# Five subtractions of the first layer's end by way of ScalarE and GpSimd, and one normalisation on VectorE

## The reference

```python
x = x + tanh(g_xattn[0]) * attention0(layernorm(x), ctx, ctx, pos, mask)   # 32 heads in 8 groups, rotary positions
x = x + tanh(g_ffn[0])   * experts0(layernorm(x))                          # 16 experts, the best 2 of each token
x = x + tanh(g_xattn[1]) * attention1(layernorm(x), ctx, mask)             # RMS-normed queries and keys
x = x + tanh(g_ffn[1])   * lora_experts1(layernorm(x))                     # 4 experts of rank 16, the best 2
# attention: q = x @ Wq; k = ctx @ Wk; v = ctx @ Wv
#            scores = q k^T / sqrt(128), masked; probs = softmax(scores); out = (probs v) @ Wo
```

## Time and profile before

| | |
|---|---|
| median of 3 runs | 1198.05 us (1197.17 to 1198.39) |
| profiled execution, its own time | 1198.88 us |
| span of its records | 1196.8 us |
| TensorE busy | 1182.5 us, 99% of the span |
| VectorE busy | 825.7 us, 69% |
| GpSimd busy | 580.8 us, 49% |
| ScalarE busy | 423.9 us, 35% |
| subtractions into `o_lo` (L1431) | 128 of 682 ns mean, all on VectorE |

### The profile page before, as it was taken

The page is one execution under the profiler, slowest core; times in us unless marked ns, Lnnn a source line. Parts: engine busy times, 40 slices in busy tenths (PEclk is TensorE's granted clock), DMA queues, the critical chain, the costliest instruction groups (busy, mean ns, idle before and its releaser), DMA issues.

```text
span 1196.8 us, 16826 instructions
## 1 busy us (share of the span) xinstructions
PE 1182.5 (99%) x6178; PEld 944.8 (79%) x6178; DVE 825.7 (69%) x1454; ACT 423.9 (35%) x746; POOL 580.8 (49%) x396
## 2 busy tenths in 40 slices
PE   9999999999999999999999999999999999999998
PEld 7888888777778777777788888777777777777776
DVE  4656546888888888888973226766676767657795
ACT  5145152222213222222451115544443343544432
POOL 5522533766767576676463112336364554545500
PEclk9999999999999999999999999999999999999999
DMA  7844635712212221211211003112221221211101
GB/s 281 260 146 166 205 112 163 282 49 79 79 53 75 83 79 45 78 45 54 88 63 36 1 1 134 40 62 71 81 87 44 79 73 59 70 53 40 75 1 71
DMA packets 57314, 106.54 MB, mean 89 GB/s; under 512 B 3632, under 2 KB 36528, under 8 KB 51888
## 3 DMA queue, kind: packets, MB, share of 16 engines
q1 hardware_dynamic: 56736, 104.82, 25.4%
q0 software_dynamic: 384, 1.05, 0.2%
q10 hardware_dynamic: 144, 0.00, 0.0%
HBM read 78.59 MB, written 27.26 MB: 88 GB/s over the span
## 4 chain that ended last, share of the span: by engine, by line
PE 89%; DVE 7%; POOL 2%; issue 1%; ACT 1%; DVEq 0%; POOLq 0%; ACTq 0%
PE ps_q L225 13%; PE ps_b L225 13%; PE ps_b L227 13%; PE ps_b L226 13%; PE ps_q L226 12%; PE ps_q L227 12%; PE ps_s L938 4%; PE ps_b L965 4%; PE ps_q L925 1%; PE ps_s L273 1%; PE ps_q L2039 1%; PE ps_b L472 1%; DVE ln_buf L265 1%; PE ps_q L522 0%; PE ps_s L1733 0%
## 5 line engine op out<-in xcount | busy, mean ns | idle before, releaser
L225 PE MATMUL ps_q<-hT_hi,wq_hi 128*128 128x512 f32 x512 | 206.3, 403 | 0.0
L226 PE MATMUL ps_q<-hT_lo,wq_hi 128*128 128x512 f32 x512 | 199.8, 390 | 0.0
L227 PE MATMUL ps_q<-hT_hi,wq_lo 128*128 128x512 f32 x512 | 199.4, 389 | 0.0
L225 PE MATMUL ps_b<-wo_hi,o_hi 128*128 128x512 f32 x440 | 171.5, 390 | 0.7 <-POOL wo_lo L1256 0.7
L226 PE MATMUL ps_b<-wo_lo,o_hi 128*128 128x512 f32 x440 | 171.2, 389 | 0.0
L227 PE MATMUL ps_b<-wo_hi,o_lo 128*128 128x512 f32 x440 | 171.2, 389 | 0.0
L1431 DVE TENSOR_TENSOR o_lo<-ps_b,o_hi 128x512 fp32r<-128x512 f32 x128 | 82.0, 682 | 63.6 <-ACT o_hi L1141 62.3
L225 PEld LDWEIGHTS ps_q<-hT_hi,wq_hi 128*128 128x128 f32 x512 | 96.0, 188 | 33.2 <-issue 11.2
L1263 POOL TENSOR_TENSOR qT<-q_t 128x512 f32<-128x512 f32 x64 | 89.9, 1405 | 65.8 <-DVE q_t L1366 59.8
L1442 DVE SCALAR_TENSOR_TENSOR x_sb<-ps_b,gates,x_sb 128x512 f32<-128x512 f32 x117 | 83.8, 723 | 43.7 <-PE ps_b L227 43.3
L731 POOL TENSOR_TENSOR wq_lo<-wq_raw,wq_hi 128x512 fp32r<-128x512 f32 x64 | 90.3, 1415 | 47.8 <-ACT wq_hi L725 47.8
(11 more groups left out here) (272 smaller groups left out, 2471.5 us busy)
## 6 DMA issues: line engine op xcount, KB each, us to landing
wq_raw<-in_wq SPq DMA_DIRECT2D x16, 1024.0 KB, 4.8
wo_raw<-in_wo SPq DMA_DIRECT2D x16, 1024.0 KB, 4.8
kT<-kT_spill SPq DMA_DIRECT2D x32, 256.0 KB, 3.7
v_hi<-v_hi_spill SPq DMA_DIRECT2D x16, 512.0 KB, 3.7
v_lo<-v_lo_spill SPq DMA_DIRECT2D x16, 512.0 KB, 4.6
v_hi_spill<-vs_hi SPq DMA_DIRECT2D x12, 512.0 KB, 5.4
v_lo_spill<-vs_lo SPq DMA_DIRECT2D x12, 512.0 KB, 6.7
kw_raw<-in_wk SPq DMA_DIRECT2D x4, 1024.0 KB, 7.1
```

The costliest lines, as they stand in the source:

```text
L225: nc.tensor.matmul(dst, l_hi, r_hi, start=first, stop=False)
L226: nc.tensor.matmul(dst, l_hi, r_lo, start=False, stop=False)
L227: return nc.tensor.matmul(dst, l_lo, r_hi, start=False, stop=last)
```

## The change

It does three things, all in the first layer's end.

- Five low parts of value banks leave VectorE: 2 and 3 of unit 13, and 0, 2 and 3 of unit 14. For each, ScalarE copies the PSUM bank into a free slot of `wo_raw` (`out_copy`, signal `o_copied`), and GpSimd subtracts `o_hi` from that copy (`out_low` of `att_pool`, signal `o_back`). Low part 1 of unit 14 and all of unit 15 stay on VectorE.
- The normalisation of unit 14 (`att_normalise`) moves from GpSimd's stream to VectorE's, right behind the reciprocal.
- The waits follow: TensorE's `project_out` counts `o_back` where it counted `o_lo`, each copy waits until its slot is free, and ScalarE's first copy of the next stage's up weights waits for all five subtractions.

```diff
+        BY_POOL = 5
...
             def project_out(u, h, g, t):
                 if t % 2 == 0:
                     pe.wait_ge(*c("o_hi", 4 * u + t + 2))
-                    pe.wait_ge(*c("o_lo", 4 * u + t + 2))
+                    at_end = u - (2 * G - 3) if lay == 0 and isinstance(u, int) else -1
+                    if at_end < 0 or (at_end, t) == (0, 0):
+                        pe.wait_ge(*c("o_lo", 4 * u + t + 2))
+                    elif (at_end, t) == (1, 0):
+                        pe.wait_ge(*c("o_lo", 4 * u - 1))
+                        pe.wait_ge(c["o_back"], 3)
+                    elif at_end == 2:
+                        pe.wait_ge(*c("o_lo", 4 * u + t + 2 - BY_POOL))
+                    else:
+                        pe.wait_ge(c["o_back"], 2 if at_end == 0 else BY_POOL)
...
+            def out_copy(u, n, slot):
+                if slot in (0, 1):
+                    act.wait_ge(c["x_part"], slot + 1)
+                elif u == 2 * G - 2:
+                    act.wait_ge(c["o_back"], 1)
+                else:
+                    act.wait_ge(*c("wo_lo", 4 * G))
+                nc.scalar.activation(wo_raw[:, slot, :].rearrange("p (t j q) -> p t j q", t=2, j=J),
+                                     ps_b[n].rearrange("p (t j q) -> p t j q", t=2, j=J), ACT.Copy).then_inc(c["o_copied"], 1)
...
             def output_copy(u, t):
...
+                if t == 2:
+                    act.wait_ge(c["o_back"], 2)
...
+            def out_low(u, n, slot, m):
+                half, par = divmod(n, 2)
+                pool.wait_ge(*c("o_hi", 4 * u + n + 1))
+                pool.wait_ge(c["o_copied"], m)
+                part = (slice(None), slice(2 * half, 2 * half + 2), slice(None), slice(par * S, (par + 1) * S))
+                nc.gpsimd.tensor_tensor(o_lo[part], wo_raw[:, slot, :].rearrange("p (t j q) -> p t j q", t=2, j=J),
+                                        o_hi[part].bitcast(F32), ALU.subtract).then_inc(c["o_back"], 1)
...
-                if do_score:
+                if do_score and not (lay == 0 and before_closing(lay, g, h)):
                     att_normalise(pool, lay, us)
...
+                out_low(2 * G - 3, 2, 3, 1)
+                out_low(2 * G - 3, 3, 2, 2)
                 for t in range(PAIRS - 1):
                     pool.wait_ge(*c("y_added", 4 * (2 * G - 3) + t + 1))
...
+                out_low(2 * G - 2, 0, 0, 3)
+                out_low(2 * G - 2, 2, 1, 4)
+                out_low(2 * G - 2, 3, 3, 5)
                 pool.wait_ge(*c("p_lo", 2 * G))
...
                 sums(last - 1)
-            out_low(last - 2, 2)
-            out_low(last - 2, 3)
+                att_normalise(dve, lay, last - 1)
             if lay:
+                out_low(last - 2, 2)
+                out_low(last - 2, 3)
                 sums(last - 1)
...
             if (w, n) == ("u", 0):
                 act.wait_ge(att[0]["x_part"], PAIRS - 1)
+                act.wait_ge(att[0]["o_back"], BY_POOL)
```

More of the change, by code:

```diff
@@ L205, in build @@
                 att_signals[name] = per_unit * units
+        att_signals["o_lo"] -= BY_POOL
         ln_signals = {"sd": 2, "rs": 2} | dict.fromkeys(("stats", "moments", "normed", "transposed", "hi", "lo"), NT)
@@ L1190, in step @@
                             exponentials(us)
+                        if lay == 0 and before_closing(lay, g, h):
+                            out_copy(up, 2, 3)
+                            out_copy(up, 3, 2)
                     if do_project and lay:
@@ L1228, in att_act @@
             out_high(last - 1, 0)
+            if lay == 0:
+                out_copy(last - 1, 0, 0)
             out_high(last - 1, 1)
@@ L1232, in att_act @@
             out_high(last - 1, 3)
+            if lay == 0:
+                out_copy(last - 1, 2, 1)
+                out_copy(last - 1, 3, 3)
             beside(0, -1)
@@ L1568, in att_dve @@
                 sums(last - 1)
-            out_low(last - 2, 2)
-            out_low(last - 2, 3)
+                att_normalise(dve, lay, last - 1)
             if lay:
+                out_low(last - 2, 2)
+                out_low(last - 2, 3)
                 sums(last - 1)
-            if lay:
                 add_output(last - 2, 1, 0)
@@ L1588, in att_dve @@
             att_shift(dve, lay, last)
-            out_low(last - 1, 0)
+            if lay:
+                out_low(last - 1, 0)
             out_low(last - 1, 1)
             sums(last)
-            out_low(last - 1, 2)
-            out_low(last - 1, 3)
+            if lay:
+                out_low(last - 1, 2)
+                out_low(last - 1, 3)
             att_normalise(dve, lay, last)
```

## The result

The changed kernel takes 1204.38 us (median of 6 runs, 1201.76 to 1205.46), the kernel before 1198.15 us (6 runs, 1197.17 to 1198.39). The ratio is 1.0048, with a 95% interval of 1.0039 to 1.0058: about 6.2 us, or 0.5%, slower. The profiled execution took 1205.16 us with a span of 1203.1, against 1198.88 and 1196.8 before. Its records lie 0.46 us ahead of those of before in this place (GpSimd's last rotation stands at 571.85, before at 572.31), so 0.46 is added where a time is compared with one of before.

A forecast was written before the change was run, and what follows sets the result against it. TensorE bounds the kernel, its waits at the first layer's end set by VectorE's chain. Jams with GpSimd make everything 5.0 us later: 1198.88 + 5.0 = 1203.9 profiled, median 0.8 lower, 1203.1 us; range 1199.5 to 1205.0.

The forecast's parts named there:

- The sum without the lock: First layer's end, each instruction at its own length, no blocking between VectorE and GpSimd: 1.8 us gain; no-jam rival, chance 0.08.
- The first jam: Unit 14's sums: VectorE's exchange and normalisation wait on GpSimd's unbroken row of four; unit 14's probabilities 3.1 us later.
- The second jam: Unit 15's maxima: VectorE's exchange waits on GpSimd's subtraction of unit 14's first low part; TensorE starts 3.4 us later than before.
- The third jam: Unit 15's sums: VectorE's small instructions wait on GpSimd's last two subtractions; normalisation ends 5.0 us later than before.
- What was costed at nothing: TensorE's project_out 13 tile 2 still starts on time after GpSimd's second subtraction, and no copy on ScalarE waits.
- The clock: Rival: TensorE's clock drops to 1.2 GHz in its longer wait ahead of unit 14's values; +1.5 us, 1204.6 us, chance 0.07.
- the long wait: TensorE standing 3.9 us ahead of unit 14's values, where it stood 0.82 us before.
- the wait of 1.5 us that I had listed: TensorE standing about 1.5 us ahead of project_out 14, from 588.0, expected to take up part of slower matmuls.
- the first rival: Jams as told but shorter, small instructions slipping past GpSimd at 1.25 us each: middle +1.9 us, 1200.0 us, chance 0.15.

The follow-up runs named there:

- e4_early_row: e1_u13_part with unit 13's two subtractions moved ahead of VectorE's exchange and GpSimd's additions waiting for the normalisation: 1197.52 us, ratio 0.9996.
- e7_held_adds: Changed kernel, but GpSimd's three additions for unit 13 wait until VectorE has normalised unit 14; its two subtractions stay: 1201.86 us, ratio 1.0034.
- e1_u13_part: Changed kernel with unit 14's three low parts back on VectorE; unit 13's two stay on GpSimd, the normalisation on VectorE: 1202.13 us, ratio 1.0036.
- e2_u14_part: Changed kernel with unit 13's low parts back on VectorE and unit 14's normalisation back on GpSimd; unit 14's three low parts stay moved: 1200.37 us, ratio 1.0023.
- e6_kept_warm: Changed kernel with unread TensorE matmuls put into its waits, 14 ahead of unit 14's values and 6 ahead of unit 15's: 1203.25 us, ratio 1.0044.
- e5_full_again: The changed kernel itself, unaltered, run again beside the later experiments: 1204.45 us, ratio 1.0055 against the kernel before.

## Why the prediction was right, step by step

The forecast was 1203.1 us in a range of 1199.5 to 1205.0; the time is 1204.38. Direction, mechanism and most of the size were right; one term stood in the wrong place and one was missing. Luck has a part in how close the number came, as told below.

- **The sum without the lock (a gain of 1.8 us).** Rightly not forecast. `e4_early_row` gets 0.6 us of it at `values` of 14 (0.23 for 0.82) and 0.4 to 0.5 in the end.
- **The first jam.** Forecast: the exchange takes 3.9 us, the normalisation is listed with 1.9 and ends 3.1 us late, TensorE stands for 3.9. Measured: 3.85, 1.86, 577.33 + 1.86 + 0.46 = 579.65 (2.99 later than 576.66), 3.81. The rule held: the first tiny instruction passes, and each further one slips in behind one of GpSimd's. `e7_held_adds` took out just what two fewer give. The Trainium skill, "SBUF — State Buffer", "Who interferes with whom", says that issue order, not the shape of the instruction, decides who blocks. The traces agree where one instruction meets one: before, VectorE's mask began 0.17 us ahead, took its 1.22 us, and GpSimd's addition took 2.20; after, the addition began 0.52 us ahead and the mask took 2.30. For a row of GpSimd they show more than that, since the waiting VectorE instruction gets in at the next boundary although GpSimd's next one is ready.
- **The second jam: right size, wrong place.** I let low part 0 of unit 14 fall on the exchange of maxima, 1.9 us; it took 0.91. Instead the mask took 2.30 us in place of 1.22, because GpSimd's third addition started at 582.21, 0.5 us ahead of it; before it came 0.17 us behind (580.39 and 580.22). The missed step is on ScalarE. Here are its rows after:

```profile
580.50 1.06 ACT L1145 ACTIVATE p_hi<-pT 128x1024 fp32r<-128x1024 f32 x1 [5.49 <-DVE pT L1469]
581.47 0.67 ACT L1171 ACTIVATE wo_raw<-ps_b,gates 128x512 f32<-128x512 f32 x1
```

  The output copy of tile 2, which feeds that addition, used to wait for TensorE after `p_hi`; the trace of before shows it thus:

```profile
577.98 1.06 ACT L1134 ACTIVATE p_hi<-pT 128x1024 fp32r<-128x1024 f32 x1 [2.49 <-DVE pT L1425]
579.63 0.69 ACT L1148 ACTIVATE wo_raw<-ps_b,gates 128x512 f32<-128x512 f32 x1 [0.58 <-PE ps_b L227]
```

  Now `p_hi` is late, TensorE has long been done, and the copy follows `p_hi` at once. It is 0.97 us behind it in place of 1.65, while the mask still follows `p_lo` by 1.14 us (582.73 − 581.59, before 580.22 − 579.08): their order turned round. That the shift ends at 588.49 + 0.46 = 588.95, where 588.8 was forecast, is partly luck: another block of nearly the same length stood in. `e1_u13_part` shows the mask's block without any subtraction for unit 14, `e2_u14_part` the one that I had forecast.
- **The third jam.** Forecast: third and fourth instruction stand, the normalisation ends at 595.7, the last addition at 600.7. Measured: 2.91 us for the four, 595.53 + 0.46 = 595.99, and 600.55 + 0.46 = 601.0.
- **What was costed at nothing.** `project_out` 13 tile 2 did not wait for GpSimd's second subtraction in the changed kernel, and no copy on ScalarE waited.
- **The clock: a term missing from the sum.** I named the drop as a rival with 0.07, far too little for what every run of the changed kernel shows, and looked at the long wait only. It happened there (0.50 from 583.5) and cost TensorE itself nothing, since the slow matmuls ran into the wait of 1.5 us that I had listed; by the later subtraction it cost 0.1 us in this profile and 0.6 in that of `e5_full_again`, a path that I had not seen. The rival's 1204.6 us lies nearer to 1204.38 than my forecast, by luck: its 1.5 us were for the drop behind the long wait. What I had not looked at is the stretch ahead of unit 15's second half of `values`, where the jams leave a wait of 1.72 us, few matmuls and another 0.29 us of waiting, with no slack behind. Unit 15's normalisation is 594.30 − 589.44 + 0.46 = 5.3 us behind that of before; the next addition of a bank of `ps_q`, which waits for TensorE, is further behind. VectorE's timeline before, and then after:

```profile
599.74 0.75 DVE L1442 SCALAR_TENSOR_TENSOR x_sb<-ps_q,gates,x_sb 128x512 f32<-128x512 f32 x1 [0.46 <-PE ps_q L227]
```

```profile
606.08 0.75 DVE L1486 SCALAR_TENSOR_TENSOR x_sb<-ps_q,gates,x_sb 128x512 f32<-128x512 f32 x1 [1.93 <-PE ps_q L229]
```

  That is 606.08 − 599.74 + 0.46 = 6.8 us: 1.5 us more, and VectorE's wait for TensorE has grown by as much (1.93 for 0.46). So the second drop costs 1.5 us in this execution. `e5_full_again`, the same program without it, has 4.76 us between its additions at 599.90 and 604.66, where this one has 6.27 (599.81 and 606.08). `e6_kept_warm` against `e5_full_again` puts the difference of the medians at 1.2, which is the effect of whatever drops the five runs of the latter had.

So the forecast of 5.0 us stands against 5.1 us of jams (`e6_kept_warm`; in its profile unit 15's normalisation begins 593.52 − 571.19 = 22.33 us after the last rotation, before 17.13, so 5.2) and 1.2 of clock, 6.3 together (1204.45 − 1198.12). No slack behind the layer's end gave anything back, as forecast. One run of the changed kernel took 1201.76 and another 1202.24, over 1 us under the rest and below even `e6_kept_warm`. A fuller clock does not explain them, for their mean granted clock is 0.997, as in the slowest of the eleven; whether a jam was shorter in them, as in the first rival, no profile shows.

## What to carry to other kernels

When work is moved from VectorE to GpSimd, don't subtract its length from the one and add it to the other: write down what GpSimd will run without a gap, and lay it beside VectorE's instructions with two inputs in SBUF, and its copies within SBUF, which were caught too (four of 32x16 in 4.64 us). Most exposed are short ones in a chain, each of which can cost a whole GpSimd instruction; a row of four made 0.77 us into 3.85. Moving the row by a few microseconds, or holding back what stands behind it, saved from 1.7 us (`e7_held_adds`, in the profile) to 4.6 us here (1202.13 − 1197.52, `e1_u13_part` and `e4_early_row`, with the same work on GpSimd), while no version with work moved to GpSimd was faster than the kernel before by more than the noise. And after any change that lengthens waits of TensorE, look for those behind which no slack is left: most of the price of a drop in its clock fell there, not at the longest wait. Where there is slack, ask what the slower matmuls delay on the other engines.

## What the runs showed of the hardware that I had not expected

- The granted clock fell to 1.2 GHz behind waits of only 1.72 and 0.29 us, with TensorE busy for 1.59 of 3.5 us (597.0 to 600.5) in the profile of the change. A stretch that looks alike in `e5_full_again`, busy for 1.69 of 3.5 us, was followed by full clock, and so were waits of 1.72 and 0.30 us in `e7_held_adds`. So the same program has the drop in some runs and not in others, and the times fall into groups up to 2.4 us apart (`e2_u14_part`).
- The price of a drop depends on what stands behind it: in one execution, 0.1 us at 583.5, where a wait of TensorE followed, and some 1.5 us at 600.6, where none did. A drop at the first place that began 0.6 us earlier against `values` cost 0.6 us, because it moved a GpSimd subtraction into VectorE's exchange (`e5_full_again`).
- Turns are kept at each boundary of GpSimd's row: in each such place that I looked at, tiny VectorE instructions with two inputs got through one at a time, 1.25 us apart, though GpSimd had its next instruction ready.
